# A new order for Pool and ScalarE in the attention steps of a fused adaLN, linear attention and MoE kernel

## The reference, cut to what matters

```python
h = layernorm(x) * (1 + ca) + sa                     # x is 8 x 2048 x 512, ca, sa, ga per batch row from silu(c) @ wmod
xn = layernorm(h) * ln_gamma + ln_beta
k, v, r = xn @ Wk.T, xn @ Wv.T, xn @ Wr.T
kv = k * v
csum = cumsum(kv * td ** t, axis=time)
wkv = tf * kv + td * shifted(csum)
x = x + ga * ((sigmoid(r) * wkv) @ Wo.T)
h2 = layernorm(x) * (1 + cb) + sb
# two groups of 32 experts: top 2 of 32 by softmax(h2 @ router), SwiGLU experts
x = x + gb * (moe0(h2) + moe1(h2)) / 2
```

## Time and profile before

| | |
|---|---|
| median of 3 runs | 5163.3 us (5159.52 to 5163.87) |
| the profiled execution | 5175.09 us, of it 5173.3 us from the first to the last instruction |
| share of the span busy | PE 90%, PEld 74%, DVE 60%, POOL 55%, ACT 31% |
| mean granted TensorE clock | 0.95 of full speed |
| stage A's 32 steps | up to about 1983 us of the span |
| the rest of stage A | to about 2105 us |
| stage C | to 5173.3 us |

### The profile page before, as it was taken

How to read it: one execution, slowest core, us unless ns; L and a number is a source line. 1 busy time by engine, 2 the same in 40 slices (tenths; PEclk the granted TensorE clock), 3 DMA queues, 4 the chain that set the end, 5 groups by cost and what they waited for, 6 DMA issues and landing times.

```text
span 5173.3 us, 89076 instructions
## 1 busy us (share of the span) xinstructions
PE 4644.2 (90%) x22649; PEld 3825.1 (74%) x22649; DVE 3124.7 (60%) x6155; ACT 1625.5 (31%) x4045; POOL 2858.7 (55%) x2301
## 2 busy tenths in 40 slices
PE   6989898989998885689889987998999999999998
PEld 4777777777777774467677776777878888888886
DVE  6898889889888885444344443454434444444443
ACT  2334333343443342123222332332222222222222
POOL 2566777776667775344344443554545555555554
PEclk8999999999999997799999998999999999999999
DMA  5545454545454452799999998999899899898887
GB/s 219 175 148 172 142 177 145 167 151 173 155 169 151 152 163 93 267 302 287 311 306 299 301 287 287 285 319 300 211 266 262 219 258 259 223 253 218 216 230 190
DMA packets 413885, 1152.42 MB, mean 223 GB/s; under 512 B 57057, under 2 KB 57058, under 8 KB 394930
## 3 DMA queue, kind: packets, MB, share of 16 engines
q0 software_dynamic: 182512, 454.27, 36.6%
q1 hardware_dynamic: 189634, 544.27, 29.2%
q10 hardware_dynamic: 41472, 151.01, 7.7%
HBM read 719.35 MB, written 463.57 MB: 229 GB/s over the span
## 4 chain that ended last, share of the span: by engine, by line
PE 32%; DMA 20%; issue 4%; POOL 2%; DVE 1%; POOLq 1%; SPq 0%; DVEq 0%; ACT 0%; ACTq 0%
DMA out<-c_yo,c_idx 19%; PE ps L1284 9%; PE ps L1286 9%; PE ps L1285 9%; PE ps L1293 3%; PE ps L1312 1%; POOL out L1275 1%; POOL c_xg L1244 1%; DMA c_wt<-wsp_d 1%; DVE c_yo L1528 1%; POOLq L1267 0%; DVE c_xl L1516 0%; DMA wsp_d<-c_stg 0%; DVE c_hTl L1521 0%; POOL c_lists L1256 0%
## 5 line engine op out<-in xcount | busy, mean ns | idle before, releaser
L1275 POOL DMA_INDIRECT out<-c_yo,c_idx x576 | 919.4, 1596 | 1067.5 <-DMA out<-c_yo,c_idx 617.8
L1284 PE MATMUL ps<-c_wt,c_xh 128*128 128x512 f32 x2304 | 967.6, 420 | 46.3 <-issue 22.9
L1286 PE MATMUL ps<-c_wt,c_xl 128*128 128x512 f32 x2304 | 911.1, 395 | 0.0
L1285 PE MATMUL ps<-c_wt,c_xh 128*128 128x512 f32 x2304 | 906.8, 394 | 0.0
L1528 DVE SCALAR_TENSOR_TENSOR c_yo<-ps,c_wc,c_xg 128x512 f32<-128x512 f32 x576 | 432.5, 751 | 730.2 <-DMA out<-c_yo,c_idx 471.0
L1244 POOL DMA_INDIRECT c_xg<-h2g_d,c_idx x576 | 569.7, 989 | 513.5 <-DVE c_yo L1528 403.2
L1512 DVE TENSOR_TENSOR c_hh<-ps,c_sil 128x256 f32<-128x256 f32 x576 | 243.8, 423 | 823.6 <-ACT c_sil L1364 756.2
L1369 ACT CAST c_xh<-ps 128x512 fp32r<-128x512 f32 x576 | 337.7, 586 | 1091.4 <-PE ps L1293 1005.0
L431 PE MATMUL ps<-xTh,wTh 128*128 128x512 f32 x1536 | 622.0, 405 | 61.7 <-DVE xTl L798 57.8
L692 POOL DMA_INDIRECT list_d<-pairs,sidx x512 | 556.0, 1086 | 215.5 <-issue 127.5
L1284 PE MATMUL ps<-c_wt,c_hTh 128*128 128x512 f32 x1152 | 468.1, 406 | 159.8 <-DVE c_hTl L1521 145.9
(11 more groups left out here) (196 smaller groups left out, 8032.3 us busy)
## 6 DMA issues: line engine op xcount, KB each, us to landing
c_wt<-wsp_d SPq DMA_DIRECT2D x69, 2048.0 KB
c_wt<-wsp_d SPq DMA_DIRECT2D x69, 1024.0 KB
sraw<-wex SPq DMA_DIRECT2D x194, 256.0 KB
wsp_d<-shigh SPq DMA_DIRECT2D x192, 256.0 KB
wsp_d<-sraw SPq DMA_DIRECT2D x192, 256.0 KB
c_stg<-wex ACTq DMA_DIRECT2D x96, 512.0 KB
wsp_d<-c_sgh ACTq DMA_DIRECT2D x96, 512.0 KB
wsp_d<-c_stg ACTq DMA_DIRECT2D x96, 512.0 KB
```

The costliest lines, as they stand in the source:

```text
L1275: nc.gpsimd.indirect_dma_start(out=out, out_offset=bass.IndirectOffsetOnAxis(ap=idx[:, n:n + 1], axis=0), in_=yo[:, n % 4, :], in_offset=N ...
L1284: nc.tensor.matmul(o, lh, rh, start=first, stop=False)
L1285: nc.tensor.matmul(o, lh, rl, start=False, stop=False)
L1286: return nc.tensor.matmul(o, ll, rh, start=False, stop=last)
```

## The change

Only the order of calls in two of the hand-written steps changes. No instruction is added or taken away.

On Pool: the last five of the 16 scatters (11 to 15) leave their step and stand near the head of the next one; the other eleven are grouped anew (7, 1, 2 and 1); `receive` of the chunks 2 and 3 and the low parts get other neighbours; the staged parts move. On ScalarE: the seven `stage_hi` move to other places, the sixth and seventh ahead of `front`; `hi(2)` moves ahead of the router's copy `logits`; `chunk_r` of chunk 3 stands between the second and the third of `front`'s four copies, no longer behind all of them.

```diff
-            def front(b, s):
-                for k in range(KC):
+            def front(b, s, ks):
+                for k in ks:
...
                 chunk_k(b, s, 0)
+                stage_hi(b, at)
+                stage_hi(b, at + 1)
                 chunk_r(b, s, 0)
                 if not (first and s < 2):
                     soften(b, s - 2)
-                stage_hi(b, at)
                 hi(b, s, 0)
-                stage_hi(b, at + 1)
+                stage_hi(b, at + 2)
+                stage_hi(b, at + 3)
                 normed(b, s)
                 chunk_k(b, s, 1)
-                stage_hi(b, at + 2)
                 chunk_r(b, s, 1)
                 chunk_k(b, s, 2)
                 if back_too:
                     turned(b, s)
                 hi(b, s, 1)
-                stage_hi(b, at + 3)
+                stage_hi(b, at + 4)
                 chunk_r(b, s, 2)
                 chunk_k(b, s, 3)
-                stage_hi(b, at + 4)
+                hi(b, s, 2)
+                stage_hi(b, at + 5)
                 if back_too:
                     logits(b, s)
-                hi(b, s, 2)
-                front(b, s)
-                stage_hi(b, at + 5)
+                stage_hi(b, at + 6)
+                front(b, s, (0, 1))
                 chunk_r(b, s, 3)
+                front(b, s, (2, 3))
                 hi(b, s, 3)
-                stage_hi(b, at + 6)
...
                 rstd(f_var, vaf, h_ready, rsf, f_rstd, b, s + 1)
+                if not (first and s < 3):
+                    scatter(b, s - 3, 11, 16)
+                stage_lo(b, at)
                 receive(b, s, 0)
-                stage_lo(b, at)
+                stage_lo(b, at + 1)
                 lo(b, s, 0)
                 rstd(g_var, vag, z_ready, rsg, g_rstd, b, s + 1)
-                stage_lo(b, at + 1)
+                stage_lo(b, at + 2)
+                stage_lo(b, at + 3)
                 if not (first and s == 0):
                     rstd(b_var, vab, h2_ready, rsb, b_rstd, b, s - 1)
                 if old:
-                    scatter(b, s - 2, 0, 4)
-                stage_lo(b, at + 2)
+                    scatter(b, s - 2, 0, 7)
                 receive(b, s, 1)
                 if old:
-                    scatter(b, s - 2, 4, 6)
+                    scatter(b, s - 2, 7, 8)
                 lo(b, s, 1)
-                stage_lo(b, at + 3)
-                if old:
-                    scatter(b, s - 2, 6, 9)
                 receive(b, s, 2)
-                if old:
-                    scatter(b, s - 2, 9, 11)
                 stage_lo(b, at + 4)
                 lo(b, s, 2)
+                stage_lo(b, at + 5)
+                stage_lo(b, at + 6)
                 if old:
-                    scatter(b, s - 2, 11, 16)
-                stage_lo(b, at + 5)
+                    scatter(b, s - 2, 8, 10)
                 receive(b, s, 3)
+                if old:
+                    scatter(b, s - 2, 10, 11)
                 lo(b, s, 3)
-                stage_lo(b, at + 6)
...
             rstd(b_var, vab, h2_ready, rsb, b_rstd, B, -1)
+            scatter(B, -3, 11, 16)
             scatter(B, -2, 0, 16)
```

More of the change, by code:

```diff
@@ L621, in step @@
                 hi(b, s, 1)
-                stage_hi(b, at + 3)
+                stage_hi(b, at + 4)
                 chunk_r(b, s, 2)
                 chunk_k(b, s, 3)
-                stage_hi(b, at + 4)
+                hi(b, s, 2)
+                stage_hi(b, at + 5)
                 if back_too:
                     logits(b, s)
-                hi(b, s, 2)
-                front(b, s)
-                stage_hi(b, at + 5)
+                stage_hi(b, at + 6)
+                front(b, s, (0, 1))
                 chunk_r(b, s, 3)
+                front(b, s, (2, 3))
                 hi(b, s, 3)
-                stage_hi(b, at + 6)
             normed(0, -1)
-            front(0, -1)
+            front(0, -1, range(KC))
             for s in range(4):
```

## The result

The changed kernel takes 5085.7 us (median of 4 runs, 5084.55 to 5087.98) against 5163.6 before in the same comparison; the ratio is 0.9847, with a 95% interval of 0.9829 to 0.9865. So it is faster, by 78 us, as forecast; but 172 us were forecast, more than twice as much, and 5085.7 lies inside the stated range (4915 to 5105) only near its end. It came out near the second rival, 5077 us.

A forecast was written before the change was run, and what follows sets the result against it. Pool's late chunk 3 product starved PE and VectorE; afterwards VectorE would be late. 29 steps from 60.3 to 54.7 us give 162, with earlier steps and tail 172 us: 4991 us, forecast 4950 to 5040, wider range 4915 to 5105.

The forecast's parts named there:

- the second rival: VectorE and Pool collide more in the stage A steps: 57.5 us per step, 5077 us in total; chance 0.13.
- The five scatters and the late product: Pool's chunk 3 product no longer waits behind five scatters (6.8 us); PE's output wait of 3.55 us per step goes whole.
- VectorE's idle time before chunk 0: ScalarE delivers chunk_k(0) on time, freeing VectorE's 2.6 us idle per step, worth something only where VectorE sets the pace.
- The stretch: VectorE instructions lengthened beside Pool's tensor products: 5.5 us per step kept unchanged, bounded at -2.8 to +2.8 us.
- The head of the step: The five moved scatters, 6.8 us, fall into Pool's idle time at the next step's start: cost nothing.
- The third step as a model: Program's third step, without either idle time, has VectorE's 54.3 us cadence; every step should become like it, mean 54.7 us.
- The instructions that stretch: L816, L775 and L825 on VectorE, two SBUF inputs each, four per step: 5.5 us of stretch in 52.9.
- The stores ahead of `front`: ScalarE's stage_hi(6) waits for part 4's stores, landing in 3 to 4 us: just in time, cost 0 to 0.5 us.
- The Wo steps: Pool's four scalings alternate with staged parts: s = 1 falls by some 10 us, the other steps by 4.
- Small terms: Outside the 29 steps: 5 us from the two earlier steps, 4.8 us from the tail of stage A.
- PE becomes the bound: Rival: VectorE without stretch needs 47 us, so PE sets 52.2 us per step, 4916 us in total; chance 0.13.
- The signs of being wrong: Wrong if ScalarE idles before L562 for a store ahead of front, or L825, L816 and L775 have longer means.

The follow-up runs named there:

- the last experiment: Kernel with eight scatters spilled, VectorE's three eps additions done as tensor_reduce: 4995.0 us, ratio 0.9660, the fastest kernel that leaves nothing out.
- eight scatters spilled: Changed kernel with scatters 8 to 15 at the next step's head, staged part 6 behind chunk 3's product and behind front on ScalarE: 5004.4 us, ratio 0.9708.

## Why the prediction was right in its way and wrong in its size

- *The five scatters and the late product.* Right. L661 of chunk 3 starts 2.9 us behind the sigmoid in the step at 1202 and the output's wait of 3.55 us per step is gone. But the gain was booked as if it went to the time. The run with the scatters alone shows that it can go into VectorE's stretch instead: 60.0 us per step for 60.3, with VectorE busy for 57.1.
- *VectorE's idle time before chunk 0.* Right that it ends. The prediction counted 2.6 us of idle time before kv, the wait for ScalarE; there were 5.5 (158.2 us in the 29 steps), some of it before chunk 3, and 5.3 of them went.
- *The stretch, "I keep the 5.5 and bound the change of place by about half of it either way".* This is the step that failed, by its size. I took the change as 0 and it was +3.0 us per step (55.9 for 52.9 us busy), just over the upper bound of +2.8 that the text had; 54.7 + 2.8 was the rival at 5077 us, which came out. With 54.7 + 3.0 = 57.7 the step would have been 0.5 us too long for the measured 57.2. The argument for zero was that the number of Pool's products doesn't change. What changed is what they lie on.
- *The head of the step, "I cost it at nothing".* Half of that growth arose here: staged part 0, behind the five scatters, lies on the `aa` of chunk 0, (2.30 - 0.74) = 1.6 us per step. With eight scatters ahead of that part this `aa` is at 0.74 again, and in the run with the scatters alone, where the part stands behind `receive(0)`, it is at 0.74 too. The prediction asked of this place only whether `receive(0)` would be late, and not what VectorE does beside it.
- *The third step as a model, 54.3 us from split to split*. It was the reason for 54.7 and it misled. From split to split VectorE was busy for 52.5 us of it, 3.4 less than in a mean step after, and Pool was busy for 31.8 us only in that step, where a mean step has 42.1. So less of Pool's work could fall on VectorE's, and the step was a favourable one. In the changed kernel the same third step takes 52.1 us again.
- *The instructions that stretch.* I counted three lines, 5.5 us. Their means over all 29 steps give 5.2, so that sum was right, partly by luck: L816 was taken by its median (1022 ns for a mean of 1262) and L825 from four steps (1308 for 1006). Four more lines were in it: L769/L771, `hit`, and the tiny vaf and vag, which have a single input. Over all lines VectorE's stretch was some 8 us per step before and 11 after. By the Trainium skill (VectorE: DVE Perf Modes, section Mode 2×_2P) a tensor_scalar from SBUF to SBUF can use both read ports for its one tensor, and by GPSIMD Engine Reference, Key points, such a form contends with Pool like one with two SBUF inputs. The traces agree: vaf 1746 ns, as a reduce 161. That the ports are the reason, no run here shows by itself.
- *The stores ahead of `front`.* The landing was forecast at 3 to 4 us; in the step shown Pool ends part 4 at 1198.4 and ScalarE goes on at 1201.4, 3.0 us later. The wait is there (131.4 us in the 29 steps) and cost some 0.4 us per step at the most, by the two runs with part 6 moved. In the step shown it also pushed Pool's part 6 onto the last `aa`, which I had not followed.
- *The Wo steps.* The means by s (batch rows 1 to 7) went from 58.3, 65.1, 58.8, 58.7 to 58.8, 57.4, 56.0, 56.9 us: s = 1 gained 7.7 (forecast 10), the others 2.8, 1.8 and a loss of 0.5 (forecast 4 each).
- *Small terms.* Steps 1 and 2: 0.6 us instead of 5. The tail to the last stage's start: 91.3 to 88.2 us, 3 instead of 5.
- *PE becomes the bound.* Not here; it took the stretch to be removed first (the last experiment, s = 2 and 3).
- *The signs of being wrong.* Both that the prediction named came true: ScalarE idles before L562 for a store, and L825 and L775 have longer means (1006 to 1538 and 1261 to 1322 ns); L816's is shorter (1262 to 1124).

## What to carry to other kernels

When the removal of a wait makes a second engine the bound, price that engine at its busy time in the new arrangement, not in the old one: idle time that lies beside another engine's work is not free to be filled. Before moving a Pool tensor operation, list what VectorE does at its new place. In these traces statistics, reduces and instructions with an operand in PSUM kept their time beside it, within 0.03 us. Instructions with two SBUF inputs (0.74 us became up to 3.8 for `aa` in the kernel before) and the tensor_scalar from SBUF to SBUF did not. The scan was stretched now and then (1.29 us, at most 2.57). A tiny instruction can be the dearest one of a step, so read mean durations against the smallest, line by line, before counting work.

## What the runs showed of the hardware

- Four-element additions on VectorE took 1746 (vaf, changed kernel) and 2668 ns (vag, eight scatters spilled) on the mean where Pool's products run, 161 ns as a tensor_reduce in the same place.
- An `aa` (two SBUF inputs, 128x512) beside a Pool product lasted 1.13 us longer on the mean in the changed kernel, and one beside none kept its 0.74 us. A bn_stats beside one kept its 0.67 us.
- Adding 2.5 us of bn_stats per step cost 0.1 us beside Pool's run of products and 2.3 us elsewhere, at a VectorE busy share of 98% in both cases. A busy share that contains stretch does not tell how much more work an engine can take.
- The granted clock of the steps went from 0.95 to 0.97 as PE's waits got shorter, and was 1.00 in the steps of the fastest kernel in which PE did not wait.
